# Inverse norms spread over the free axis: GpSimd and TensorE, or two small DMAs through DRAM

## The reference

```python
z_l = h @ W_lang.T;  z_g = h @ W_grav.T;  v = h @ W_V.T
zn  = z_l / maximum(norm(z_l), EPS)
A_l = maximum(zn @ zn.T, 0) * not_eye
d2  = maximum(sq + sq.T - 2 * z_g @ z_g.T, 0)
A_g = exp(-d2 / (2 * sigma**2)) * not_eye
K   = w_l * row_stochastic(A_l * mask) + (1 - w_l) * row_stochastic(A_g * mask)
out = layernorm(x + (K @ v) @ W_O.T)
```

## Time and profile before

| | |
|---|---|
| Time, median of 3 runs | 773.46 us (773.16 to 773.95) |
| The profiled execution's own time | 773.02 us |
| Its span, first to last instruction | 771.3 us |
| PE busy | 95% of the span |
| DVE, ACT, POOL busy | 63%, 45%, 16% |
| Granted TensorE clock, mean | 0.987 |
| DMA queue of SP and ACT, share of 16 engines | 24.5% |

### The profile page before, as it was taken

One profiled execution on the slowest core, in us unless ns is written; L12 is line 12 of the kernel. 1 busy time (PEld: TensorE's weight loads), 2 busy tenths in 40 slices (PEclk: granted clock), 3 DMA queues, 4 the chain that ended last, 5 costly groups with the idle time before them and its releaser, 6 DMA issues.

```text
span 771.3 us, 11265 instructions
## 1 busy us (share of the span) xinstructions
PE 732.2 (95%) x3436; PEld 602.1 (78%) x3436; DVE 485.9 (63%) x1328; ACT 349.9 (45%) x647; POOL 121.3 (16%) x336
## 2 busy tenths in 40 slices
PE   6599999999999999999999999999999999999984
PEld 5478878878787878878787887878787887878772
DVE  3634675747576674857667574757677584766472
ACT  4423344443544554454544444354455444354443
POOL 0000201111210201121120211121020111112031
PEclk9899999999999999999999999999999999999997
DMA  9302014031231414022231404023141402220111
GB/s 286 109 0 56 1 55 110 28 109 28 82 82 54 109 52 111 27 80 56 82 82 54 109 27 118 18 82 82 54 109 54 109 27 94 42 82 28 55 54 56
DMA packets 54976, 55.00 MB, mean 71 GB/s; under 512 B 3504, under 2 KB 36528, under 8 KB 54960
## 3 DMA queue, kind: packets, MB, share of 16 engines
q1 hardware_dynamic: 54688, 54.28, 24.5%
q10 hardware_dynamic: 272, 0.52, 0.2%
HBM read 38.01 MB, written 16.78 MB: 71 GB/s over the span
## 4 chain that ended last, share of the span: by engine, by line
PE 66%; DVE 12%; ACT 11%; issue 8%; DMA 1%; POOL 1%; ACTq 0%; DVEq 0%; POOLq 0%
PE bank L757 60%; ACT p_hi L405 3%; PE bank L855 3%; DVE hT_lo L525 3%; ACT hT_hi L359 2%; PE bank L779 2%; ACT y L434 2%; ACT junk_a L428 2%; DVE work L611 2%; DVE hT_raw L519 1%; DVE kt_lo L654 1%; DVE work L618 1%; DVE y L662 1%; ACT work L418 1%; DVE p_lo L589 1%
## 5 line engine op out<-in xcount | busy, mean ns | idle before, releaser
L757 PE MATMUL bank<-hT_lo,m_hi 128*128 128x512 f32 x512 | 179.9, 398 | 1.5 <-DVE wvo_lo L554 1.5
L589 DVE TENSOR_TENSOR p_lo<-bank,p_hi 128x512 fp32r<-128x512 f32 x128 | 87.7, 685 | 65.0 <-ACT p_hi L405 63.6
L757 PE MATMUL bank<-hT_hi,m_lo 128*128 128x512 f32 x320 | 125.1, 391 | 0.0
L757 PEld LDWEIGHTS bank<-hT_lo,m_hi 128*128 128x128 f32 x512 | 96.3, 188 | 20.4 <-issue 1.9
L405 ACT CAST p_hi<-bank 128x512 fp32r<-128x512 f32 x128 | 74.1, 579 | 67.9 <-PE bank L757 67.9
L757 PE MATMUL bank<-wvo_hi,hT_hi 128*128 128x512 f32 x256 | 102.6, 401 | 0.0
L757 PE MATMUL bank<-p_hi,hT_hi 128*128 128x512 f32 x256 | 101.4, 396 | 1.0 <-DVE p_lo L589 1.0
L757 PE MATMUL bank<-wvo_hi,hT_lo 128*128 128x512 f32 x256 | 100.1, 391 | 0.0
L757 PE MATMUL bank<-p_lo,hT_hi 128*128 128x512 f32 x256 | 100.0, 391 | 0.0
L757 PE MATMUL bank<-wvo_lo,hT_hi 128*128 128x512 f32 x256 | 99.7, 390 | 0.0
L409 ACT COPY xs<-bank 128x512 f32<-128x512 f32 x64 | 37.2, 582 | 113.4 <-PE bank L757 113.4
(11 more groups left out here) (101 smaller groups left out, 1246.0 us busy)
## 6 DMA issues: line engine op xcount, KB each, us to landing
x_blk<-in_x SPq DMA_DIRECT2D x128, 128.0 KB, 3.4
x_nat<-in_x SPq DMA_DIRECT2D x32, 512.0 KB, 3.3
out_y<-y SPq DMA_DIRECT2D x32, 512.0 KB, 2.8
work<-in_L_gnn_W_grav SPq DMA_DIRECT2D x2, 512.0 KB, 6.6
work<-in_L_gnn_W_V SPq DMA_DIRECT2D x2, 512.0 KB, 8.3
y<-in_L_gnn_W_O SPq DMA_DIRECT2D x2, 512.0 KB, 7.4
work<-in_L_gnn_W_lang ACTq DMA_DIRECT2D x1, 512.0 KB, 5.3
work<-in_L_gnn_W_lang SPq DMA_DIRECT2D x1, 512.0 KB, 4.9
```

What stands on the lines that cost most here:

```text
L589: nc.vector.tensor_tensor(dst, src, hi.bitcast(F32), ALU.subtract).then_inc(proj_ready, 1)
L757: last = pe.matmul(dst, lhsT, rhs, start=(n == 0), stop=(n == len(steps) - 1))
```

## The change

`rnorm[:, b]`, 128 partitions of two floats, is written to a DRAM scratch `r_spill[b]` (1 KB), SP waits for it to land, and a second DMA reads that 1 KB back into each of the 128 partitions of `r_row[:, b]` (128 KB in all). `cosine_masked` waits for this second DMA (`r_loaded[b]`) and reads `r` from SBUF, with a stride of two floats, since the two node tiles are interleaved there. The products into `r_wide` on POOL, the `r_turn` transposes on PE and the tile of ones are gone. On SP the loads of the blocks move ahead of `load_x` and `store`.

```diff
-        r_wide = sb("r_wide", [P, 2, NT, P])
+        r_row = sb("r_row", [P, 2, P, NT])
+        r_spill = nc.dram_tensor("r_spill", [2, P, NT], F32)
...
+            def spread_r(p, b):
+                sp.wait_ge(pool_steps, upto(p, 6, 3 * b + 1))
+                sp.dma_start(r_spill[b], rnorm[:, b]).then_inc(r_saved, 16)
+                sp.wait_ge(r_saved, 16 * (2 * p + b + 1))
+                sp.dma_start(r_row[:, b], r_spill[b].partition_broadcast(P)).then_inc(r_loaded[b], 16)
+
             def pair(p, last=False):
+                spread_r(p - 1, 1)
+                if not last:
+                    sp.wait_ge(turned, upto(p, 2, 4))
+                    load_blocks(p + 2)
                 for b in range(2):
                     sp.wait_ge(y_ready, upto(p - 1, 4, 2 * b + 2))
                     load_x(p, b)
                     store(p - 1, b)
-                if not last:
-                    sp.wait_ge(turned, upto(p, 2, 4))
-                    load_blocks(p + 2)
+                spread_r(p, 0)
+
+            spread_r(0, 0)
...
+            spread_r(PAIRS - 1, 1)
             for b in range(2):
                 store(PAIRS - 1, b)
...
-                pool.wait_ge(pool_steps, done + 1)
-                for t in range(NT):
-                    nc.gpsimd.tensor_tensor(r_wide[:, b, t], ones[:], rnorm[:, b, t:t + 1].broadcast_to([P, P]),
-                                            ALU.mult).then_inc(r_ready, 1)
...
-                dve.wait_ge(rcol_done, upto(q, 2, b + 1))
-                nc.vector.tensor_tensor(wk_t(b, RADJ), gg_bank[:, 0:N].unsqueeze(1).broadcast_to([P, NT, N]),
-                                        adj_off[:], ALU.mult).then_inc(radj_ready, 1)
+                dve.wait_ge(r_loaded[b], 16 * (q + 1))
+                nc.vector.tensor_tensor(wk_t(b, RADJ).rearrange("p t (u m) -> p t u m", u=NT),
+                                        r_row[:, b].rearrange("p m u -> p u m").unsqueeze(1).broadcast_to([P, NT, NT, P]),
+                                        adj_off[:].rearrange("p t (u m) -> p t u m", u=NT),
+                                        ALU.mult).then_inc(radj_ready, 1)
...
-            def r_turn(q, b):
-                pe.wait_ge(r_ready, upto(q, 4, 2 * b + 2))
-                pe.wait_ge(gram_ready, upto(q, 4, 2 * b + 2))
-                for t in range(NT):
-                    last = pe.transpose(gg_bank[:, t * P:(t + 1) * P], r_wide[:, b, t], ident[:])
-                last.then_inc(rcol_done, 1)
```

More of the change, by code:

```diff
@@ L84, in gnn_resnorm @@
         ident = sb("ident", [P, P])
-        ones = sb("ones", [P, P])
         junk_d = sb("junk_d", [P, 2, NT, P])
         junk_a = sb("junk_a", [P, NT, D])
-        r_wide = sb("r_wide", [P, 2, NT, P])
+        r_row = sb("r_row", [P, 2, P, NT])
+        r_spill = nc.dram_tensor("r_spill", [2, P, NT], F32)
         x_diag = sb("x_diag", [P, 2, 2, NT])
@@ L121, in wk_t @@
             return work[:, b, what, :].rearrange("p (t n) -> p t n", t=NT)
-        CONSTANTS = ((ones, 1.0), (half, 0.5), (minus_half, -0.5), (floor, EPS), (one_by_d, 1.0 / D),
+        CONSTANTS = ((half, 0.5), (minus_half, -0.5), (floor, EPS), (one_by_d, 1.0 / D),
                      (minus_one_by_d, -1.0 / D), (eps_row, EPS), (ln_eps_row, LN_EPS))
@@ L171, in gnn_resnorm @@
         norm2_ready = sem("norm2_ready")
-        r_ready = sem("r_ready")
+        r_saved = sem("r_saved")
+        r_loaded = [sem(f"r_loaded{b}") for b in range(2)]
         pool_steps = sem("pool_steps")
@@ L175, in gnn_resnorm @@
         gram_ready = sem("gram_ready")
-        rcol_done = sem("rcol_done")
         radj_ready = sem("radj_ready")
@@ L900, in pair @@
                     k_times_v(q, 0, 1, y_ready, upto(q, 4, 1))
-                    r_turn(q, 1)
                 project(p, parity, 5, first)
@@ L922, in pair @@
                 value(p, parity, 1, 1)
-                r_turn(p, 0)
                 x_tile(p, parity, 1, 0)
@@ L947, in _ @@
             gram_turn(p, 1, L)
-            pe.wait_ge(radj_ready, upto(p, 2, 1))
+            pe.wait_ge(gram_ready, upto(p, 4, 2))
             gram_turn(p, 1, G)
@@ L952, in _ @@
             k_turn(p, 0)
-            r_turn(p, 1)
             pe.wait_ge(proj_ready, upto(p, PV, PV))
```

## The result

The changed kernel takes 831.15 us (median of 4 runs, 828.31 to 831.58), against 773.31 us before on the same chip: a ratio of 1.0743, with a 95% interval of 1.0719 to 1.0766. The predicted 769.7 us, and its range up to 780.5, are missed by 50 us and more.

The account below looks back on a forecast made before the run. PE was taken to bound each period's first half, DVE/ACT the second. From 773.02 us, 16 x 0.23 off gave 769.3; the median's 0.4 us above the profiled execution made 769.7 us, range 764.8 to 780.5.

Parts of the forecast that it names:

- the arrival of r: First batch of a pair: write lands at 347.9, read takes 2.3 us, `r_row` there at 350.3; DVE waits about 0.7 us.
- The bound from above: Write of `rnorm` behind the store: at most a whole transfer again, the shortest in the trace, 2.3 us, landing at 349.5.
- the slack: PE before `k_turn`, first batch: `kernel_sum` can come 1.2 us later without PE waiting, so DVE's 0.7 us fits in.
- the last pair: Store issued at 738.10, `r` 5.6 us later at 743.7; the multiply stood at 744.28, so the transfer is hidden.
- 351.5: Arrival of the first batch's `r` by the Trainium skill's fixed 2.0 us: write lands at 349.1, read takes 2.0 + 0.3.
- The price past that point: Past an arrival at 350.8, every 0.1 us costs PE 0.1 us in each of the loop's 14 pairs.
- The transposes: Each `r_turn` on PE costs 0.23 us; the 16 in the first half count, 3.7 us off, the second ones nothing.
- I leave it there: DVE's multiply by the mask, now reading `r` from SBUF instead of PSUM, stays at 0.68 us.
- if the multiply itself gets longer: Stated sign of being wrong: a longer multiply by the mask on DVE would delay `kt_lo` in the second half too.
- Rival 1: Slow 8-byte writes or slow read: `r` arrives at 351.5, PE waits 0.7 us a pair; 779.5 us, chance 0.24.
- Moving the loads, the second batch's DMAs and their traffic: On SP: earlier block loads cost nothing; second batch has over 6 us of cover for 1.6 + 2.3 us of transfers.
- rival 3: On PE the second transposes count too, all 32 `r_turn`s, 7.4 us off: 766.1 us, chance 0.09.

## Why the prediction was wrong

**The step that failed is the arrival of r:** "it lands at 347.9, and SP issues the read at 348.0" and "I take that: `r_row` is there at 350.3". The write was given 2.7 us behind the store, the read 2.3. In pieces of 64 bytes or more I would have been near: 2.5 and 2.9. In pieces of 8 bytes the write took 3.6 to 5.7 us and the read 2.9 to 4.6, and from the store's issue to the landing of `r` went 8.3 to 9.2 us in the loop. I had said that no such write was in the trace, and still took the value nearest to my guess. The bound from above, a whole small transfer, wasn't one either: even with it I reached 8.3 us from the store's issue, and in the pair shown it was 9.1. Behind a store there was no way to hide this; ahead of it there was, since the slack, 1.2 us, was right. In the last pair, where I had `r` hidden, DVE waited 2.2 us for it.

The 2.0 us of the Trainium skill, "DMA: Bandwidth & Descriptors", section "Anatomy of one DMA", from which I had worked out 351.5, are given there for DMAs that GpSimd issues; mine are issued by SP. By that figure the write was to land 1.9 us after the store's last bytes; I had taken 0.7, and in the pair shown it was 3.4 (366.0 to 369.4). A write in 64-byte pieces with nothing ahead took 1.4 us from issue to landing, less than 2.0.

**The price past that point was right for the wait and left out the clock.** I booked 0.1 us for each 0.1 us late. In the first batches of the loop DVE waited 3.8 us in the mean and PE 2.6, which is 3.8 less the slack. In the mean period of the changed kernel 4.06 us were added: 44.07 - 43.92 = 0.15 remain without any wait for `r`, 46.61 - 44.07 = 2.54 are the wait with the clock kept up, and 47.98 - 46.61 = 1.37 the clock. Up to 0.2 of the 1.37 may be the wait again, since DVE waited 3.5 us for `r` in the run with the ten products, not 3.8. The third term was in no rival.

**The transposes.** 0.23 us for an `r_turn` was right, and so was that only those in the first half count: the period with one of the two left in place is 43.68, 0.24 below 43.92.

**"I leave it there" for the multiply was right in its own duration** (0.68 and 0.69 us) **and wrong in what it does to its neighbour.** In the second half, which DVE, POOL and ACT bound, `minus_mean` is on the chain, and it took 0.38 us more. This alone turns the forecast gain of 3.7 us into no change: 0.15 us a period more instead of 0.23 less. I had named "if the multiply itself gets longer" as a way to be wrong; it was the instruction beside it. The Trainium skill, "SBUF — State Buffer", section "SBUF: two separate sides", has this rule: a DVE instruction with two operands in SBUF and a GpSimd instruction that reads SBUF share a port pair, which one of them holds to its end while the other is blocked. By that rule the trace agrees, 0.58 against 0.20 us, and the old multiply, with one operand in PSUM, left `minus_mean` alone.

**The rivals.** Rival 1 named the mechanism, slow landing of 8-byte writes and a slow read, and its place, but at 779.5 us its size was off by the factor that the clock and 9.1 instead of 6.8 us make. Moving the loads, the second batch's DMAs and their traffic were free, as forecast. Nothing speaks for rival 3: with both `r_turn`s gone the period was 44.07 us, which one of them and the 0.38 of `minus_mean` make up.

What stays open: why pieces of 8 bytes land so late. That they are slow is shown, the mechanism isn't. The Trainium skill, "DMA: Bandwidth & Descriptors", section "Specifications", says that transfers under 512 bytes are done by reading, changing and writing back. No such limit is seen in these landings: 64 bytes took what 512 took.

## What to carry to other kernels

Before a transfer takes the place of an on-chip path, count the size of its pieces as well as its bytes, ask what stands ahead of it in its queue, and compare the sum with the slack of the instruction that needs it. A wait of two or three microseconds on TensorE costs more than itself when the clock falls behind it; here useless work in the gap was cheaper than the gap. Compare the periods of the loop, too, and not the medians alone: the end of a program can be faster or slower by its own clock. Moving an operand from PSUM to SBUF on DVE can leave its own time alone and still delay a GpSimd instruction that runs beside it.

## What the runs showed of the hardware that I had not expected

- A DRAM write of 128 pieces of 8 bytes, 1 KB, mostly lands 2.8 to 3.3 us after its issue with nothing ahead (4.4 once in the loop), and after 3.6 to 5.7 us behind a 512 KB store; pieces of 64 or 512 bytes land in 1.4 and 1.5 us free, and in 2.4 to 2.6 us behind the store.
- The store ahead of such a write is held up too: its own landing, 2.8 us as a rule, took 4.1 to 6.1 us in 5 of the loop's 14 pairs, and never over 2.9 with pieces of 64 bytes behind it.
- A read of 1 KB by 128 partitions, 2.9 us behind pieces of 64 or 512 bytes, takes 4.0 us in the median behind 8-byte pieces of the same 1 KB. Reading elsewhere it took 2.9 us with no store ahead, and 3.6 behind one.
- After a wait of 2.9 us TensorE was granted 0.50 of its clock for 3.6 us, and 22 products took 7.4 us; ten useless products in the gap kept it at 1.00. The clock fell after 10 of 14 such waits, and their length alone doesn't tell which: it fell after one of 2.14 us and stayed up after one of 2.84.
- A GpSimd instruction of 0.20 us took 0.58 beside a DVE multiply of 0.69 us with both operands in SBUF, in all 15 places, and 0.20 where the multiply had one operand in PSUM.
